# Chunk 1's layer 0 directly behind chunk 0's, projections of chunks 1 to 3 among the first units, four clears by DMA from a zero tile

## What is computed

```python
qkv = (_ln(x, g1, be1) @ w_qkv + b_qkv).reshape(b, t, 3, h, dh)      # layer 0
ckv = (context @ w_ckv + b_ckv).reshape(b, s, 2, h, dh)
k, v = concat(k_self, k_ctx), concat(v_self, v_ctx)                   # 128 keys a query
attn = softmax(where(causal | context, q @ k * scale, -inf))
x = x + attn @ v
hdn = gelu(_ln(_ln(x, g2, be2), gf, bf) @ w1 + b1)
x = x + (hdn @ w2 + b2)
Q, K, V = _layer_norm(x) @ wq.T + bq, ctx @ wk.T + bk, ctx @ wv.T + bv  # layer 1
out = softmax(where(key_mask == 0, NEG_INF, Q @ K / sqrt(hd))) @ V @ wo.T + bo + x
```

## Time and profile before

| | |
|---|---|
| median of 3 runs | 466.83 us (463.14 to 469.13) |
| the profiled execution | 466.68 us, span 464.7 us |
| busy share of the span | PE 83%, DVE 63%, ACT 56%, POOL 31% |
| mean granted clock of TensorE | 0.920 |

### The profile page before, as it was taken

How to read it: one execution, slowest core, us unless ns; L and a number is a source line. 1 busy time by engine, 2 the same in 40 slices (tenths; PEclk the granted TensorE clock), 3 DMA queues, 4 the chain that set the end, 5 groups by cost and what they waited for, 6 DMA issues and landing times.

```text
span 464.7 us, 20173 instructions
## 1 busy us (share of the span) xinstructions
PE 385.1 (83%) x8885; PEld 280.0 (60%) x8885; DVE 293.5 (63%) x733; ACT 261.3 (56%) x451; POOL 142.3 (31%) x209
## 2 busy tenths in 40 slices
PE   3759969996989898979999798969898989587674
PEld 1337747664576666757676667657676677355463
DVE  5435786469569775797469665876389549506331
ACT  2467735653757477555746475646656756435241
POOL 7100634046205520462116320551047106502000
PEclk9975997999999899998999899999899999888856
DMA  6758076017602650185105830284001400310200
GB/s 190 200 152 165 8 183 161 1 70 173 172 4 106 146 165 3 72 171 150 49 13 147 191 91 2 95 172 128 2 26 39 129 1 27 106 34 26 71 25 23
DMA packets 41958, 42.86 MB, mean 92 GB/s; under 512 B 3192, under 2 KB 34376, under 8 KB 41872
## 3 DMA queue, kind: packets, MB, share of 16 engines
q1 hardware_dynamic: 40420, 39.86, 33.3%
q0 software_dynamic: 624, 1.26, 1.0%
q10 hardware_dynamic: 828, 0.46, 0.3%
HBM read 23.65 MB, written 17.83 MB: 89 GB/s over the span
## 4 chain that ended last, share of the span: by engine, by line
PE 53%; DVE 17%; ACT 11%; issue 9%; POOL 5%; DMA 2%; ACTq 1%; SPq 0%; DVEq 0%; POOLq 0%
PE dense L667 12%; PE dense L690 7%; DVE top L971 6%; PE dense L680 4%; PE mixed L850 4%; PE key L820 3%; PE dense L672 3%; PE key L811 3%; PE mixed L858 3%; ACT probs L504 3%; PE side L883 3%; PE query L778 2%; PE query L770 2%; ACT hidden L588 2%; PE dense L662 2%
## 5 line engine op out<-in xcount | busy, mean ns | idle before, releaser
L971 DVE TENSOR_REDUCE top<-query 128x8 f32<-128x1024 f32 (+1 forms) x96 | 117.3, 1222 | 77.0 <-PE query L778 57.2
L504 ACT ACTIVATE probs<-key 128x1024 f32<-128x1024 f32 x96 | 98.3, 1024 | 85.3 <-PE key L820 58.6
L444 POOL TENSOR_TENSOR top<-top 128x8 bf16<-128x8 f32 (+1 forms) x96 | 20.3, 213 | 224.6 <-DVE top L971 223.8
L820 PE MATMUL key<-top_row,spread 48*64 48x128 bf16 x1536 | 48.8, 227 | 2.8 <-ACT top_row L509 1.8
L850 PE MATMUL mixed<-probs,v 128*32 128x128 f32 x1024 | 42.1, 283 | 0.0
L437 POOL TENSOR_TENSOR rstd_x<-var_eps_x,half 128x4 f32<-128x4 f32 x24 | 24.5, 1020 | 55.9 <-DVE var_eps_x L948 55.9
L811 PE MATMUL key<-q_stack,k_stack 48*64 48x128 f16 x1024 | 41.0, 223 | 0.0
L525 ACT COPY o_t<-mixed 128x256 f32<-128x256 f32 x96 | 35.3, 368 | 9.5 <-PE mixed L871 5.1
L667 PE MATMUL dense<-normed_ft,w 128*128 128x512 f32 x64 | 33.5, 647 | 6.4 <-ACT normed_ft L545 5.1
L820 PEld LDWEIGHTS key<-top_row,spread 48*64 48x64 bf16 x1536 | 33.8, 110 | 5.8 <-ACT probs L504 4.1
L509 ACT COPY top_row<-mixed 128x128 bf16<-128x128 bf16 x96 | 27.0, 281 | 15.9 <-PE mixed L871 15.9
(11 more groups left out here) (116 smaller groups left out, 774.0 us busy)
## 6 DMA issues: line engine op xcount, KB each, us to landing
...
scratch_k<-k_part SPq DMA_DIRECT2D x16, 256.0 KB, 2.6
scratch_q<-q_part SPq DMA_DIRECT2D x16, 256.0 KB, 2.6
...
x_in<-in_x SPq DMA_DIRECT2D x8, 256.0 KB, 3.5
...
```

Of the source, the lines that this page charges most:

```text
L504: nc.scalar.activation(probs[u.number % 2][:].rearrange("p h q -> p (h q)"), key[:].rearrange("p h x -> p (h x)"), ACT.Exp, scale=SCALE).t ...
L820: ins = nc.tensor.matmul(key[T * n:T * n + T, h, a * P:(a + 1) * P], spread[u.layer][rows, A2 * h + a, T * n:T * n + T], top_row[u.number ...
L971: nc.vector.tensor_reduce(maxima, query[:].rearrange("p h x -> p (h x)").rearrange("p (a k) -> p a k", a=w), AX_X, ALU.max, negate=True).t ...
```

## The change

The slots are now given by lists, one entry a chunk. With the eight chunks they are L0 = 0, 8, 20, 32, 44, 56, 68, 80 and L1 = 28, 40, ..., 112; so layer 0 of chunk 1 follows chunk 0's without a gap, chunks 2 to 7 and all of layer 1 come four slots earlier, and the program has four slots fewer; slots 16 to 19 alone have no unit. The input jobs have a list of their own, IN = 0, 17, 25, 36, then as L0: chunk 1's `ctx_t` to `q0` are at slots -5 to -1 and its `v0a`, `v0b` at 1 and 3; chunk 2's `ctx_t` to `q0` at 3 to 7, chunk 3's at 14 to 18. The `x2` list has chunk 0's norm, `x2_t` and `q1` one slot earlier. The weight transposes move from slot -5 to slot 1. Four of ACT's six clears become four transfers of 1 MB that SP issues in slot 4 from a new tile of zeros (cleared by DVE); ACT does its other two behind `spread`; POOL's wait moves from slot 3 to slot 9. `x2` gets a fourth buffer, `mix_t` a second.

```diff
-SLOTS = 12
-L0_AT = (0, 1, 2, 3, 4, 5, 6, 7)
-L1_AT = (32, 33, 34, 35)
-BACK_AT = (35, 39)
-FIRST, END = -24, SLOTS * (CHUNKS - 1) + 44
+L0 = [0, 8] + [12 * c - 4 for c in range(2, CHUNKS)]
+L1 = [12 * c + 28 for c in range(CHUNKS)]
+IN = [0, 17, 25, 36] + L0[4:]
+K1, X2 = L0, [-1] + L0[1:]
+V0A, V0B = [s - 16 for s in IN], [s - 14 for s in IN]
+V1 = [s + 11 for s in L0]
+BACK_AT = (3, 7)
+FIRST, END = -24, L1[-1] + 12
...
-def due(rel, s):
+def due(rel, s, start=L0):
...
-        x2 = many(3, "x2", [P, TILES, D])
+        x2 = many(4, "x2", [P, TILES, D])
...
-        mix_t = sb("mix_t", [P, TOK])
+        mix_t = many(2, "mix_t", [P, TOK])
...
+        zeros = sb("zeros", [P, TOK])
...
-                      q_stack[1][:].bitcast(F32).rearrange("p a s x -> p (a s x)"),
-                      q1_stack[0][:].bitcast(F32).rearrange("p a s x -> p (a s x)"),
+                      q_stack[1][:].bitcast(F32).rearrange("p a s x -> p (a s x)")]
+        dma_clears = [q1_stack[0][:].bitcast(F32).rearrange("p a s x -> p (a s x)"),
...
+                if s == 4:
+                    sp.wait_ge(s_clear_dve, N_DVE_CLEARS)
+                    for n, dst in enumerate(dma_clears):
+                        sp.dma_start(dst.rearrange("p (n x) -> p n x", x=TOK), zeros[:].unsqueeze(1).broadcast_to(
+                            [P, 2 * CB * H * VW // TOK // 2, TOK])).then_inc(s_clear_v1 if n % 2 else s_clear_q1, 16)
...
-                    if c < 2:
-                        sp.wait_ge(s_clear_act, 2 * c + 3)
...
-                if s == 3:
-                    pool.wait_ge(s_clear_act, len(act_clears))
+                if s == 9:
+                    pool.wait_ge(s_clear_v1, 32)
                     for n, dst in enumerate(v1_ones):
                         nc.gpsimd.memset(dst, 1.0).then_inc(s_ones, 1)
                         pool.wait_ge(s_ones, n + 1)
+                    pool.wait_ge(s_clear_q1, 32)
...
-                if s == -5:
+                if s == 1:
                     pe.wait_ge(s_late, N_LATE)
```

More of the change, by code:

```diff
@@ L644, in _ @@
                                    cst[:, C_S1:C_S1 + H].unsqueeze(2).broadcast_to([P, H, T])).then_inc(s_spread, 1)
+                    for dst in act_clears:
+                        clear(dst)
         @block.tensor
@@ L734, in dense @@
                 for c in job_due("out", s):
-                    pe.wait_ge(s_side_read, side_number("back", SLOTS * c + BACK_AT[1]))
-                    by_tokens("out", c, mix_t, w_t[:, 3, :])
+                    pe.wait_ge(s_side_read, side_number("back", L1[c] + BACK_AT[1]))
+                    by_tokens("out", c, mix_t[c % 2], w_t[:, 3, :])
                 for c in job_due("q0", s):
```

98 lines of the change are left out of this document (51 added, 47 removed).

## The result

The changed kernel takes 484.76 us as the median of four runs (478.41 to 486.64), the kernel before 467.20 beside it. The ratio is 1.028 (1.021 to 1.036): slower by 2.8%, where I had forecast 462.3 us and no measurable change. (Ratios here compare executions at a like TensorE clock only, so they aren't the quotient of the medians.) The profiled execution took 478.41 us against 466.68, 11.7 more.

The account below looks back on a forecast made before the run. PE was taken as the bound wherever there are units. The terms -6.7 + 5.7 - 6.1 + 0.75 + 1.5 + 0.5 gave -4.35, so 466.68 us became 462.3, with a range of 453.5 to 473.

Parts of the forecast that it names:

- step 4: Empty group before chunk 2: moved work mostly fits PE's idle time, a longer DVE and POOL chain adds 2.5; net +0.75 us.
- fuller gain: Rival for the whole kernel: late inputs and new stalls cost nothing, PE keeps full clock; 456 us, chance 0.20.
- no gain: Rival: DVE and POOL needed the empty slots anyway, and the feed-forward norm makes PE wait; 467 us, chance 0.20.
- step 5: Chunk 1's units: POOL's pieces now lie between two `split_top` and stall PE, +1.5 us, ends 0 and +4.
- Unit 0 sooner: Start: unit 0's `by_query` comes at 26.7 us instead of 33.42, set by the fill; -6.7 us.
- The moved work: Chunk 0's units: chunk 1's input work and the weight transposes now stand among them on PE; +5.7 us.
- Slots 8 to 11: The empty slots go, -12.0 us, but the PE work that stood in them stays, +5.9; at worst net -3.9.
- Late input: Chunk 2's `x_in` and `ctx_in` land late, with little margin before PE's `ctx_t`; +0.5 us, range 0 to +3.
- The clears: Four clears by transfer on SP's queue, 12 us at 340 GB/s, done at 62 before POOL needs them; 0 us.
- slower, 470 us and more: Rival: slow clears hold POOL in slot 9, and behind it the fifth unit's `split_top` and PE; chance 0.10.
- The last test in my list: From chunk 3 on, every unit should stand the same distance earlier, 4 to 5 us.

Follow-up runs that it names:

- The three pairs: The changed kernel, f2 and g2, each set against a version with the slots of before (no merge); those versions took 476.74, 477.14 and 470.10 us.
- g2: f2 with POOL's ones and mask rows in slot 7 instead of 9; 477.35 us median, too scattered for a ratio.
- g1: Changed kernel with the slots of before, clears as POOL memsets, POOL's ones in slot 3, chunk 2's input loaded early; 470.10 us, ratio 1.002.
- e2: Changed kernel with DVE's reads of finished banks ahead of the maxima and norms in slots 17 and 18; 480.51 us, ratio 1.015.
- g4: g1 with chunk 1's input jobs back at their slots of before, ahead of unit 0; 470.35 us median, ratio 0.988.
- f4: Changed kernel with POOL's three operations of chunk 1's layer norm cut to one column; 477.93 us, ratio 1.023.
- e1: Changed kernel with chunk 2's `x_in` and `ctx_in` issued right behind chunk 0's fills; 478.84 us, ratio 1.016.
- e5: Changed kernel with chunk 1's input jobs back at their slots of before, ahead of unit 0; 482.36 us, ratio 1.028.
- f1: Changed kernel with the four clears as POOL memsets ahead of the units instead of transfers; 479.20 us, ratio 1.026.
- h2: g2 with POOL's three operations of chunk 1's layer norm cut to one column; 473.60 us, ratio 1.011.
- f2: Changed kernel with the four clears as POOL memsets and chunk 2's `x_in` and `ctx_in` issued early; 479.98 us, ratio 1.030.

## Why the prediction was wrong

**What failed is step 4, +0.75**, and the reading under it: that an empty group costs PE's idle time in it, 3.9 us, so that the 4.85 us of work moved there would fit into idle time and only a chain of 2.5 us be added. Between unit 16 and unit 20 my steps give the merge +5.6 us at most (2.5, and 3.1 of work moved behind). The three pairs show +13.1, +14.0 and +16.7. PE's idle time there, which the moved work was to fill, didn't shrink but grew, by 6.9, 7.4 and 6.2 us. The stretch from unit 16 to unit 20, of g2 and of g1:

```profile
89.70:133.96 44.26, 32.71 (x436) 21.98 (x438) 26.23 (x69) 18.70 (x29) 11.41 (x15) 0.85 0.39 98
103.92:131.47 27.55, 22.19 (x420) 14.15 (x416) 21.29 (x56) 15.72 (x26) 13.59 (x16) 1.00 0.67 174
```

PE's busy time (the second number) grew by 10.5 us, by the moved work and by the lower clock together, and its idle time by 6.2.

I had seen that DVE was full in the empty groups (10.3 and 11.7 of 12.0 us) and called it a reason against the fuller gain only. The rival "no gain" named this mechanism ("time that DVE and POOL needed anyway"); I set it aside because the same norm costs PE nothing in full cycles. (Its sum, +0.3, was also too low for what it says: with step 5 at its own upper end of 4 it is +1.8.) In a full cycle, units give PE something to do while DVE works; in slots 16 to 19 nothing does. But DVE's sum of work isn't shown to be the bound: DVE was busy 15.3 of 17.8 us in slots 16 to 19 and 26.2 of 44.3 from unit 16 to unit 20. What the traces show is a ring, in which PE, DVE and POOL wait for each other by turns: PE for a bank, for a maximum, for `top`, and DVE for PE's `by_query` or for ACT's half of `k_ctx`. e2 took most of one wait out, and it came back as two others.

1. *Unit 0 sooner, -6.7:* right. 27.42 instead of 26.7, waiting for the fill as described, so -6.0. Its worth at unit 29 is nil or less (g1 against g4: +3.6).
2. *The moved work, +5.7:* too high where most of it lies. From unit 0's first matmul to unit 5's `exp` after took 17.8 us and before 17.6, though `x_t`, `k0`, `q0`, the weight transposes and `v0a` now stand in it: PE's clock was 1.00 from 34 to 46 us in after, where before had 0.50 from 35 to 45. The loss came between units 5 and 6 (9.8 us against 2.8), by `v0b`, the pause and the half clock behind it. The pause stood in no step: PE's instructions came late behind the fills, 1.4 to 3.7 us. So at unit 6 after was 1.2 us behind before, where steps 1, 2 and 6 together gave 0.5 ahead.
3. *Slots 8 to 11, -12.0 + 5.9:* right. From unit 6 to unit 16 the merge gained 10.1 to 10.5 us in the three pairs, where my steps give 9.45 (12.0 - 5.9 + 4.85 - 1.5). Against before, after gained only 5.4 there; of the 4.1 that it falls short of my 9.45, some 3.4 are POOL's ones, under step 5.
4. *The group before chunk 2, +0.75:* the term that failed, as above. Slots 16 to 19 took 17.8 us (I had 14.5) and slots 20 to 31 54.0 (51.7). I had counted DVE's and POOL's new work there as +2.5 and forgotten PE's side: `w2b` and `k0`, put where PE is otherwise idle, wait for each other's bank through a busy DVE (3.48 us), and `k1` waits for `w2a`'s through one that is itself waiting (2.02 us). And chunk 0's x2 norm fell beside chunk 1's POOL products: 3.52 us for what takes 1.1 in f4, where the products are cut, and that is nearly the length of the three together. The Trainium skill (SBUF — State Buffer, SBUF: two separate sides) describes an exclusive lock, held for whole instructions, between GpSimd and a DVE instruction with two SBUF inputs or in a two-port mode. The trace agrees in size, for an instruction with one tensor and two per-row scalars as inputs. I had quoted that rule and attached it to step 5, to the upper end only, without looking which DVE instruction would stand beside the products in the new order.
5. *New stalls in chunk 1's units, +1.5:* too low. PE waited 2.29 + 0.72 us for POOL's `top` and 0.70 for DVE's, and the clock was 0.66 as a mean over 10 us; g2 puts the ones and mask rows at 3.4. My "about 2 us of slack" was the slack before, when PE had an empty group to fall back to.
6. *Late input, +0.5:* PE waited 2.87 us, inside my range of 0 to 3, and SP issued `x_in` at 42.15 as worked out (42.2). But the time isn't to be had by mending it alone (e1), since the other pause lies under it.
7. *The clears, 0:* right for this kernel, and by luck in part: in e5, with chunk 1's inputs at their slots of before, PE pauses beside them. They were over at 60 to 61 us and ran at some 390 GB/s (I had 62 at 340), before POOL's slot 9, and in f1, without them, the time is the same. Two stretches of after:

```profile
53.00:54.00 1.00, 1.00 (x30) 0.74 (x30) 0.00 (x0) 0.00 (x0) 0.00 (x0) 0.50 1.05 391
58.00:59.00 1.00, 1.00 (x29) 0.76 (x22) 0.93 (x3) 0.79 (x1) 0.00 (x0) 1.00 1.05 389
```

The Trainium skill (DMA: Bandwidth & Descriptors, Where 436 GB/s comes from) gives 435 GB/s for this kind; the trace shows some 10% less with other traffic among it. The rival "slower, 470 us and more" gave the right side for a wrong reason, slow clears.

The last test in my list, that from chunk 3 on each unit stands the same distance away, held with the sign turned: 11.5 later at unit 29, 11.9 at 41, 11.0 at 65, 10.3 at 96. My range reached to 473 because all upper ends were added up, but each upper end was a guess at one wait, and none was for the case that the work of two empty groups meets in one.

**What stays open.** How the 13 to 17 us between units 16 and 20 divide beyond PE's busy and idle parts. POOL's products are some 4 of them (f4, h2). The bank hand-overs are 5.5 by the waits (the same in after, f1, f2, g2, f4 and h2), but a wait taken out isn't time gained, as e2 shows for 3 us of them. The rest, moved work, half clock and the order of DVE, is not told apart. Whether g4 beats the kernel before isn't settled: its interval lies under 1, but its median (470.35) does not differ from that of the runs beside it (469.83). No version was shown to beat before.
